# A DLRM tower in eight parts of 256 samples instead of four of 512, on one Trainium2 core

## The reference, cut to what matters

```python
# B = 2048 samples, F = 32 tables, D = 64
e = jnp.stack([tbl_f[ids[:, f]] for f in range(32)], axis=1)     # (2048, 32, 64)
z = jnp.sum(e, axis=-1)                                          # 32 sums a sample
outer = jnp.einsum('bpd,pde,bpe->bp', e[:, II], kernels, e[:, JJ])   # 496 pairs i < j, one 64x64 kernel each
h = jnp.concatenate([z, outer, dense_ctx], axis=1)               # 32 + 496 + 16 = 544
h = jnp.maximum(h @ W_top1 + b_top1, 0.0)                        # 512
h = jnp.maximum(h @ W_top2 + b_top2, 0.0)                        # 256
y = h @ W_top3                                                   # 1
```

## Time and profile before

| what | value |
|---|---|
| median of 3 runs | 955.99 us (955.94 to 958.36) |
| the profiled execution | 958.0 us |
| its span, first to last instruction | 956.2 us |
| PE busy | 841.2 us (88%), 4112 passes |
| POOL busy | 713.1 us (75%) |
| DVE busy | 613.4 us (64%) |
| ACT busy | 562.1 us (59%) |
| mean granted TensorE clock | 0.964 of 2.4 GHz |

### The profile page before, as it was taken

How to read it: one execution, slowest core, us unless ns; L and a number is a source line. 1 busy time by engine, 2 the same in 40 slices (tenths; PEclk the granted TensorE clock), 3 DMA queues, 4 the chain that set the end, 5 groups by cost and what they waited for, 6 DMA issues and landing times.

```text
span 956.2 us, 16224 instructions
## 1 busy us (share of the span) xinstructions
PE 841.2 (88%) x4112; PEld 297.9 (31%) x4112; DVE 613.4 (64%) x579; ACT 562.1 (59%) x4209; POOL 713.1 (75%) x1542
## 2 busy tenths in 40 slices
PE   0133789999994999999899999999999999999998
PEld 0011223333332333333333333333333333333333
DVE  0032468688883556588787574788787565688850
ACT  0100067788960266778882285888781475788952
POOL 6888888888888888888888888888888887600000
PEclk9976799999998999999999999999999999999999
DMA  9411111111111111111111111101111111000000
GB/s 347 129 21 22 22 22 22 21 23 22 22 22 22 23 22 21 22 24 22 22 22 22 20 22 24 21 21 21 20 21 22 22 21 21 15 1 1 1 1 0
DMA packets 19813, 28.46 MB, mean 30 GB/s; under 512 B 8901, under 2 KB 9413, under 8 KB 18825
## 3 DMA queue, kind: packets, MB, share of 16 engines
q0 software_dynamic: 16384, 16.81, 9.1%
q1 hardware_dynamic: 3336, 10.63, 3.0%
HBM read 27.40 MB, written 0.01 MB: 29 GB/s over the span
## 4 chain that ended last, share of the span: by engine, by line
PE 72%; POOL 17%; ACT 5%; issue 3%; DMA 3%; DVE 0%; POOLq 0%
PE m_ps L529 30%; PE acc L557 16%; POOL gathered L265 11%; PE m_ps L544 10%; ACT turned L355 4%; POOL x_half L235 3%; PE tr L487 3%; PE tr L457 3%; PE tr L477 2%; DMA gathered<-in_tbl,idx 2%; POOL x_fold L243 2%; PE tr L481 2%; PE tr L474 1%; PE m_ps L477 1%; PE tr L493 1%
## 5 line engine op out<-in xcount | busy, mean ns | idle before, releaser
L265 POOL DMA_INDIRECT gathered<-in_tbl,idx x512 | 490.2, 957 | 103.3 <-POOL x_fold L243 72.1
L417 DVE TENSOR_TENSOR prod<-m_ps,x_t 128x1024 f32<-128x1024 f32 x384 | 458.3, 1218 | 142.3 <-PE m_ps L531 87.6
L355 ACT ACTIVATE turned<-turned 128x64 f32<-128x64 f32 x2048 | 490.1, 242 | 77.3 <-DVE turned L430 71.5
L529 PE MATMUL m_ps<-x_t,k_sb 64*128 64x512 f32 x768 | 399.6, 630 | 5.5 <-ACT x_t L306 3.6
L531 PE MATMUL m_ps<-x_t,k_sb 64*128 64x512 f32 x768 | 400.0, 631 | 0.0
L355 ACT ACTIVATION_READ_ACCUMULATOR turned<-turned 128x1 f32 x2048 | 386.3, 189 | 0.0
L529 PEld LDWEIGHTS m_ps<-x_t,k_sb 64*128 64x128 f32 x768 | 133.3, 192 | 217.0 <-issue 173.8
L557 PE MATMUL acc<-prod,sel 128*32 128x512 f32 x1536 | 186.5, 604 | 0.0
L430 DVE TENSOR_TENSOR turned<-m_ps,gathered 128x1024 f32<-128x1024 f32 x128 | 155.8, 1218 | 43.4 <-PE m_ps L544 35.8
L235 POOL TENSOR_TENSOR x_half<-gathered 128x32 f32<-128x32 f32 x512 | 134.1, 262 | 13.1 <-DMA gathered<-in_tbl,idx 3.2
L544 PE MATMUL m_ps<-k_sb,x_t 64*128 64x512 f32 x512 | 138.7, 618 | 3.8 <-DVE turned L430 3.8
(11 more groups left out here) (38 smaller groups left out, 160.9 us busy)
## 6 DMA issues: line engine op xcount, KB each, us to landing
gathered<-in_tbl,idx POOLq DMA_INDIRECT x512
k_sb<-in_kmat SPq DMA_DIRECT2D x7, 1024.0 KB, 14.3
w_sb<-in_w SPq DMA_DIRECT2D x1, 1280.0 KB
k_sb<-in_kmat SPq DMA_DIRECT2D x2, 256.0 KB, 4.1
k_sb<-in_kmat SPq DMA_DIRECT2D x1, 512.0 KB, 6.7
w_sb<-in_w SPq DMA_DIRECT2D x1, 512.0 KB
idx<-in_ids SPq DMA_DIRECT2D x1, 256.0 KB, 2.8
z_sb<-in_dense_t SPq DMA_DIRECT2D x4, 32.0 KB
```

Of the source, the lines that this page charges most:

```text
L265: nc.gpsimd.indirect_dma_start(out=gathered[:, t, G % GR, f * D:(f + 1) * D], out_offset=None, in_=tables[2 * (STAGES - 1 - a) + f], in_of ...
L355: last = nc.scalar.activation(row, row, ACT.Copy, accum_out=z_turned[:, t, 16 * c + n:16 * c + n + 1])
L417: nc.vector.tensor_tensor(prod[:, r % PR, :, :], m_ps[:, p % MR, :, :], other, ALU.mult).then_inc(prod_ready, 1)
L529: nc.tensor.matmul(m_ps[:, p % MR, 0, :], k_sb[0:D, at, :], x_t[0:D, (q * STAGES + a0) % XR, :], start=True, stop=True)
```

## The change

- The samples are cut into 8 parts of 256 (2 tiles). A stage has 4 gathers; there are still 512 gathers in the same order of stages, with the tiles and tables of a stage in another order.
- An even step holds two doubles of 256 samples, so a part has 48 even steps and 16 turned ones, and the kernel as many steps of each kind as before (384 and 128). Each pass of an even step, of `reduce` and of the layers has 256 moving columns instead of 512, and there are twice as many of them. A turned step is what it was. Four even steps make a group of `reduce`, which has 32 passes instead of 16.
- `tr` is one bank seen as two halves of 256: from part 1 on two stages are transposed and copied at once, and two blocks of layer 1, or both of layer 2. Fillings stand before other steps, among them block pair 1 of layer 1 and stages 10 and 11 ahead of the same step (12).
- `gathered` holds 16 stages, `x_t` 32, `prod` 8, `turned` 3. The wait for a count of products is gone from the gathers; what remains is that the slot is free: its stage of the part before was transposed and, for stages 4 to 15, its turned products are done.
- ACT sums a turned step in two halves, two and three steps behind. `y` has a tile of its own.

The diff, cut to its core:

```diff
-NQ = 4
+NQ = 8
-GR = 12
-FR = 8
-XR = 18
+GR = STAGES
+XR = 2 * STAGES
-PR = 7
-BR = 2
+PR = 8
+BR = 3
...
-TURNED_AFTER = [16 + 49 * _i // 20 for _i in range(NT)]
+TURNED_AFTER = [8 + 49 * _i // 20 for _i in range(NT)]
...
+STAGES_AT_ONCE = [1] + [2] * (NQ - 1)
 AHEAD = {}
 for _a in range(STAGES):
+    AHEAD.setdefault((0, max(0, FIRST[_a] - 1)), []).append(("x", 0, _a))
+AHEAD.setdefault((0, NE - 2), []).append(("s", 0, 0))
 for _q in range(1, NQ):
+    AHEAD.setdefault((_q, 4), []).append(("t", _q - 1, 0))
+    for _n in range(H1 // P // 2):
+        AHEAD.setdefault((_q, 8 + 4 * _n), []).append(("h1", _q - 1, _n))
+    AHEAD.setdefault((_q, 17), []).append(("h2", _q - 1, 0))
+    AHEAD.setdefault((_q, 23), []).append(("y", _q - 1, 0))
+    for _a in range(0, STAGES, 2):
+        _s = NE * (_q - 1) + min(39 + 16 * _a // 5, NE + FIRST[_a] - 3)
+        AHEAD.setdefault(divmod(_s, NE), []).append(("x", _q, _a))
+    AHEAD.setdefault((_q, 43), []).append(("s", _q, 0))
...
-        m_ps = pb("m_ps", [P, MR, 2, QB])
-        acc = pb("acc", [P, QB])
-        tr = pb("tr", [P, QB])
+        m_ps = pb("m_ps", [P, MR, 2, 512])
+        acc = pb("acc", [P, 512])
+        tr = pb("tr", [P, 2, 256])
...
                 if n == 0 and G >= GR:
-                    old_q, old_a = divmod(G - GR, STAGES)
-                    pool.wait_ge(tr_filled, place("x", old_q, old_a))
+                    pool.wait_ge(tr_filled, place_of_stage(q - 1, a))
                     pool.wait_ge(x_halved, (G - GR + 1) * GATHERS)
-                    if old_a // COLS:
-                        pool.wait_ge(prod_ready, old_q * NS + LAST_TURNED[old_a // COLS] + 1)
-                if q:
-                    pool.wait_ge(prod_ready, step_of_gather(q, a) + n)
+                    if a // COLS in LAST_TURNED:
+                        pool.wait_ge(prod_ready, (q - 1) * NS + LAST_TURNED[a // COLS] + 1)
...
-                nc.scalar.activation(x_t[:, G % XR, :], tr[:], ACT.Copy).then_inc(tr_kept, 1)
+                nc.scalar.activation(x_t[:, slot(q, a):slot(q, a) + n, :], tr[:, 0:n, :], ACT.Copy).then_inc(tr_kept, 1)
...
+            def sums_due(step):
+                for f in (1, 0):
+                    q, at = divmod(step - SUM_BEHIND[f], NS)
+                    if 0 <= q < NQ and STEPS[at][0] == "turned":
+                        sum_turned(q, STEPS[at][1], f)
...
-                nc.vector.tensor_tensor(prod[:, r % PR, :, :], m_ps[:, p % MR, :, :], other, ALU.mult).then_inc(prod_ready, 1)
+                nc.vector.tensor_tensor(prod[:, r % PR, :, :].rearrange("p u (e n) -> p u e n", e=2),
+                                        m_ps[:, p % MR, :, :].rearrange("p u (e n) -> p u e n", e=2),
+                                        other, ALU.mult).then_inc(prod_ready, 1)
...
-                nc.tensor.matmul(m_ps[:, p % MR, 0, :], k_sb[0:D, at, :], x_t[0:D, (q * STAGES + a0) % XR, :],
-                                 start=True, stop=True)
-                nc.tensor.matmul(m_ps[:, p % MR, 1, :], k_sb[D:P, at, :], x_t[D:P, (q * STAGES + a1) % XR, :],
-                                 start=True, stop=True).then_inc(unit_done, 1)
+                for n, (a0, a1, _, _) in enumerate(EVEN[e]):
+                    nc.tensor.matmul(m_ps[:, p % MR, 0, n * QB:(n + 1) * QB], k_sb[0:D, at + n, :], x_t[0:D, slot(q, a0), :],
+                                     start=True, stop=True)
+                    last = nc.tensor.matmul(m_ps[:, p % MR, 1, n * QB:(n + 1) * QB], k_sb[D:P, at + n, :], x_t[D:P, slot(q, a1), :],
+                                            start=True, stop=True)
+                last.then_inc(step_done, 1)
...
-                for n in (2 * g, 2 * g + 1):
-                    _, row = row_of(n)
-                    pe.wait_ge(prod_ready, q * NS + STEP_OF["even", 2 * n + 1] + 1)
+                for e in range(GROUP * g, GROUP * (g + 1)):
+                    row = e % QUADS_OF_BLOCK
+                    pe.wait_ge(prod_ready, q * NS + STEP_OF["even", e] + 1)
                     for c in range(4):
-                        last = nc.tensor.matmul(acc[c * 32:c * 32 + 32, :], sel[:, 30 - 2 * row:62 - 2 * row],
-                                                prod[:, (q * ND + 2 * n + c // 2) % PR, c % 2, :],
+                        n, u = divmod(c, 2)
+                        last = nc.tensor.matmul(acc[c * 32:c * 32 + 32, 0:QB], sel[:, 30 - 2 * row:62 - 2 * row],
+                                                prod[:, (q * NE + e) % PR, u, n * QB:(n + 1) * QB],
```

More of the change, by code:

```diff
@@ L72 @@
 NK = _n
[L75 to L89, removed]
+LAST_TURNED = {c: max(STEP_OF["turned", i] for i in range(NT) if TURNED[i // TILES][0] == c) for c, _ in TURNED}
+QUADS_OF_BLOCK = 16
+GROUPS_OF_BLOCK = QUADS_OF_BLOCK // GROUP
 NB = NG // GROUPS_OF_BLOCK
@@ L363, in _ @@
             act.wait_ge(small_loaded, 48)
             for q in range(NQ):
-                for s in range(NS):
-                    for what in AHEAD.get((q, s), ()):
-                        keep(*what)
-                    if s in KEEP_Z:
-                        keep_z(q, KEEP_Z[s])
-                    if q and s == KEEP_LAST_Z:
-                        keep_z(q - 1, NB - 1)
-                    sum_behind(q * NS + s - SUM_BEHIND)
-            for step in range(NQ * NS - SUM_BEHIND, NQ * NS):
-                sum_behind(step)
+                for s, (kind, n) in enumerate(STEPS):
+                    if kind == "even":
+                        for what in AHEAD.get((q, n), ()):
+                            keep(*what)
+                        if n in KEEP_Z:
+                            keep_z(q, KEEP_Z[n])
+                        if q and n == KEEP_LAST_Z:
+                            keep_z(q - 1, NB - 1)
+                    sums_due(q * NS + s)
@@ L375, in _ @@
+            for step in range(NQ * NS, NQ * NS + max(SUM_BEHIND)):
+                sums_due(step)
             keep_z(LAST, NB - 1)
@@ L488, in layer2, with layer3 @@
                                             start=(c == 0), stop=(c == H1 // P - 1))
-                last.then_inc(done, 1)
-            def layer3(to, done):
+                return last
+            def layer3(to):
                 for c in range(H2 // P):
@@ L520, in multiply @@
-            def multiply(q, d):
-                p, at, (a0, a1, _, _) = q * NS + STEP_OF["even", d], K_AT["even", d], DOUBLES[d]
+                    pe.wait_ge(tr_kept, place("h1", q, 1))
+                    for c in range(2):
+                        last = layer2(c, tr[:, c, :])
+                    last.then_inc(tr_filled, 1)
+                else:
+                    pe.wait_ge(tr_kept, place("h2", q, 0))
+                    layer3(tr[0:1, 0, :]).then_inc(tr_filled, 1)
+            def multiply(q, e):
+                p, at = q * NS + STEP_OF["even", e], K_AT["even", e]
@@ L568, in _ @@
                         continue
+                    for what in AHEAD.get((q, n), ()):
+                        fill(*what)
                     multiply(q, n)
```

278 lines of the change are left out of this document (133 added, 145 removed).

## The result

| measurement | changed kernel, us | kernel before, us | ratio, 95% interval |
|---|---|---|---|
| the first | 982.22 (977.94 to 988.64, 4 runs) | 957.17 (4 runs) | 1.0263 (1.0201 to 1.0326) |
| the second | 917.26 (917.13 to 917.54, 5 runs) | 957.41 (9 runs) | 0.9582 (0.9567 to 0.9597) |
| the third | 937.84 (935.69 to 942.32, 4 runs) | 955.20 (7 runs) | 0.9819 (0.9778 to 0.9859) |
| the fourth | 916.15 (914.98 to 917.64, 4 runs) | 957.50 (7 runs) | 0.9577 (0.9557 to 0.9597) |
| the fifth | 985.43 (984.77 to 987.01, 4 runs) | 956.40 (7 runs) | 1.0301 (1.0274 to 1.0327) |

Each row is one measurement: runs of both kernels made together on one chip. The first is the result that the prediction of 922.5 us is held against, and by it the change makes the kernel 2.6% slower, outside the predicted range. The other four are later measurements of the same kernel, unedited.

The account below looks back on a forecast made before the run. PE bounds the kernel after a start waiting for gathers: 161.6 + 7 x 105.9 = 902.9, adjusted by -1.6 and +2.1 to 903.4, plus a tail of 19.1, gives 922.5 us; range 895 to 955.

Parts of the forecast that it names:

- P: Period of one part of 256 samples: 101.5 us of PE work plus 4.4 of waits, 105.9; bounds 102.4 to 109.8.
- the term of the waits: PE's waits in a part: half of 9.2 is 4.6, with opposing edits taken to cancel, so 4.4 us.
- Rival B: Reduces' shorter passes don't come at half the time, limited by PE's instruction intake; +20 us a part, middle about 985; 11%.
- The start: PE's last wait for gathers falls at 170.1 us, giving part 1 an effective start of 161.6; gain 26 us.
- the tail: Last part's layers running by themselves: halved passes and shorter copies cut 32.9 us to 19.1, a gain of 13.8.
- The new wait behind block 3 of layer 1: Blocks 2 and 3 and stages 10 and 11 precede one step, so PE waits while ACT empties the bank: 1 to 1.5 us.
- the passes of 256 columns: In even steps and reduces, a pass of half the columns takes half the time, 0.2137 us, its weight loading hidden.
- The prediction's split of the gain: 26 us at the start, 13.8 in the tail, less 4.6 over the parts and 1.6 of stages moved to the start.
- Rival C: ACT becomes the bound during turned steps, 93 us where PE needs 86; P 109.5 to 112, 948 to 966 us; 8%.
- the rule of the Trainium skill's page: Weight loads overlap matmuls only where row groups differ; 107 ns for 128 columns, some 37 us more a part, so a loss.
- costs PE nothing: The pacing of the gathers costs PE nothing in the kernel before, so its removal alone brings nothing.

Follow-up runs that it names:

- free executions: Executions of the unedited changed kernel in the second and fourth measurements, 917.26 and 916.15 us, with nearly all records of semaphore increments present.
- step 1: Kernel before, with rows of passes of 512, 256 and 128 columns added behind its end with nothing beside them: 3.44, 1.73 and 0.87 us.
- held execution: The slower way the unedited changed kernel came out: first and fifth measurements, 982.22 and 985.43 us, and in weaker form the third, 937.84 us.
- the run of 1469 us: Changed kernel without GpSimd's halving and folding of gathered rows, in the fifth measurement: 1469.07 us, ratio 1.5335 to the kernel before.

## Why the prediction was wrong, and where it was right

**The step that failed** is the length of a part, P = 105.9 with bounds of 102.4 and 109.8, and in it the term of the waits: 4.4 us were taken where a part of the first measurement has 115.5 - 101.5 = 14.0. No rival had it. Rival B's mark is there: the elements of a reduce end 1.55 us apart in places where the sum had 0.43. But B priced a limit that the passes always meet, and in free executions the same passes keep 0.43, alone they keep their pace down to a quarter of the columns (step 1), and the excess isn't of reduces only. What the runs show in place of the 4.4 us is this: **in a held execution PE gets on badly while gathers are issued and land.** That is when the time is lost; why, they do not show. Three readings bear it out. First, the last part, in which no more than a few gathers are left: from its first block of layer 1 to the end of the span it takes 109.06 us in the first measurement, 109.14 in the second (915.5 - 806.36), 109.1 in the third (934.8 - 825.70), 109.15 in the fifth (983.5 - 874.35), and 109.1 in the run of 1469 us (1468.9 - 1359.82). Held or free, it is the same to 0.1 us, and the parts with gathers take 115.5, 105.0, 108.5 and 116.0 in the four measurements. Second, the 31 us of windows above. Third, the dose: with halving and folding between two gathers (1.57 us apart) PE's rows of the first measurement have 25 stops of "issue" before even steps, 26.7 us in all and 2.6 at most, and a part is 10.5 us longer than a free one; with gathers 1.25 us apart and nothing between, a part takes 181.7 us (833.42 to 1015.07) where the free run of the same kernel takes 105.0 (364.01 to 469.01), 77 more. Its 64 gathers at 1.25 us fill 80.

The first blocks of layer 1 of the last part in the third, the fifth and the run of 1469 us:

```profile
825.70 1.03 PE L475 MATMUL tr<-z_sb,w_sb 128*128 128x256 f32 x4
...
874.35 1.03 PE L475 MATMUL tr<-z_sb,w_sb 128*128 128x256 f32 x4
...
1359.82 1.03 PE L467 MATMUL tr<-z_sb,w_sb 128*128 128x256 f32 x4
```

**What else was forecast holds.** The start and the tail hold in either kind, the period in the free kind only. This is the free second measurement: the last long wait for a gather, three first blocks of layer 1 and the last of them, PE's timeline:

```profile
169.74 1.08 PE L452 MATMUL tr<-ident,gathered 128*128 128x128 f32 x4 [2.27 <-DMA gathered<-in_tbl,idx]
```

```profile
176.36 1.03 PE L475 MATMUL tr<-z_sb,w_sb 128*128 128x256 f32 x4
...
281.36 1.03 PE L475 MATMUL tr<-z_sb,w_sb 128*128 128x256 f32 x4
...
386.36 1.03 PE L475 MATMUL tr<-z_sb,w_sb 128*128 128x256 f32 x4
...
806.36 1.03 PE L475 MATMUL tr<-z_sb,w_sb 128*128 128x256 f32 x4
```

- The start: the last long wait ends at 169.74 (170.1 predicted; 310.0 before).
- The period: 105.0 us for each of six parts (105.9 predicted), one window of it below: PE busy for 103.97. The waits are 3.5 instead of 4.4.

```profile
176.36:281.36 105.00, 103.97 (x929) 65.79 (x928) 76.00 (x80) 70.94 (x532) 91.48 (x197) 1.00 0.11 23
```

- The new wait behind block 3 of layer 1 is there, once a part, at the low end of the 1 to 1.5 us given for it; the passes of 256 columns are 0.21 us apart, and a reduce of 32 is 1.93 us long (1.9 predicted):

```profile
193.71 0.63 PE L452 MATMUL tr<-ident,gathered 128*128 128x128 f32 x4 [1.02 <-ACT h_sb L294]
```

```profile
349.65 0.38 PE L529 MATMUL m_ps<-x_t,k_sb 64*128 64x256 f32 x1
...
349.86 0.38 PE L529 MATMUL m_ps<-x_t,k_sb 64*128 64x256 f32 x1
...
353.98 1.93 PE L559 MATMUL acc<-prod,sel 128*32 128x256 f32 x32
```

- The tail, 19.1 predicted: from the end of the last reduce, 892.84 + 3.66 = 896.5, to 915.5 it is 19.0, and 18.9 in the first measurement.

```profile
892.84 3.66 PE L559 MATMUL acc<-prod,sel 128*32 128x256 f32 x64
...
903.94 3.72 PE L475 MATMUL m_ps<-z_sb,w_sb 128*128 128x256 f32 x16 [0.47 <-ACT z_sb L316]
908.23 3.72 PE L481 MATMUL m_ps<-h_sb,w_sb 128*128 128x256 f32 x16 [0.56 <-ACT h_sb L369]
912.51 1.02 PE L487 MATMUL tr<-h_sb,w_sb 128*1 128x256 f32 x4 [0.56 <-ACT h_sb L373]
```

With P = 105.0 the forecast's sum is 922.5 - 6.3 = 916.2, and the free median is 916 to 917. (The prediction's split of the gain has 4.6 us given back over the parts; its own terms make 3 x (2 x 105.9 - 210.5) = 3.9. The sum does not use that figure.) Rival C is out: ACT is busy for 70.9 of 105. Of the rule of the Trainium skill's page "TensorE: Matmul & The Clock Gate" ("The mechanism" and "LDWEIGHTS"), by which the prediction estimated some 37 us more for a part, nothing shows: in the free executions even steps, transposes and reduces keep the pace of their columns (0.21 us for a pass of 256).

**What stays open.** Why an execution is held or free: it keeps for a measurement and changed on one chip. Whether the recording of the profile has a part in it: every time here is of an execution that was recorded, records are missing in every held trace and hardly any in the free ones, and they are missing while gathers land, which is also when PE is late. The records may be lost by the way of running that holds PE, or writing them may be what holds it. No run here tells these apart, and a time of the same kernel without a profile would. The loss of records alone does not set the loss of time: the third measurement lacks as many as the first. By what PE is held is open too: its waits and increments or its operands; halving the waits and increments of the reduces did not help, and passes like theirs beside gathers were tried in a free measurement only. And why the kernel before is not touched. Its trace of the first measurement lacks records as well (5967 of the 8192 for the landings are there, and DVE's products wait 18.1 us with "issue" in 27 places, none in the version with split reduces from a free measurement), yet its parts take 210.5 us against 210.75 in that version. It differs in half the number of passes and in the pace of its gathers; the split reduces were never measured in a held execution, and the changed kernel with a pace put back was not tried. So the forecast's sentence that taking away the pacing "costs PE nothing" is shown for the free kind alone.

## What to carry to other kernels

When two kernels of different measurements are to be compared, run the unedited one again beside them first: without that control a difference is soon explained that is not in the code. A busy engine whose rows are modelled can look well while it is late; ask the engines that wait for it and the times of its semaphore increments. "Issue" or "remote" as the releaser of long waits on several engines at once can mean that records of increments are missing: count them before a cause is read out of the word, and do not take it for lost time, since the kernel before has it and loses none. And when a change gains by 4% in one way of running and loses 3% in the other, while the kernel before is the same in both, say both numbers.

## What the runs showed of the hardware that was not expected

- The same program with the same inputs took 893.5 us in one measurement and 1469 us in another on the same chip, within 0.5% inside each.
- In the slower of these, PE's rows have 0.26 us of work in 31 us in which GpSimd issued 25 indirect DMAs without a pause, and 31.00 us of work over 26 of them in the other. The changed kernel too, held or free, takes the same 109 us to 0.1 once the gathers are over.
- The traces of held executions lack records of semaphore increments: 4659, 4731 and 4837 of 8192 for the landings of the gathers, and 1704 in the run of 1469 us, against 8138 or more in every free one. After the last gather none of PE's is missing.
- fp32 passes of a reduce keep to their columns: 3.44, 1.73 and 0.87 us for sixteen matmuls of 512, 256 and 128, with a load of 32 columns of weights ahead of each.
